# Recurrent attention and expert layer on one core: the last four expert tiles leave the pass over token order

## The reference

```python
xn = _layernorm(x)
# s: delta-rule linear attention, 4 heads, dk 128, dv 64
#    S = S + k_t (beta_t (v_t - k_t^T S))^T ;  o_t = q_t^T S
#    o = rmsnorm(o) * norm_w * silu(xn @ Wg) ;  s = o @ Wo
# f: mixture of 8 experts, each token goes to the one with the largest logit
#    h = square(relu(xn @ fc[e])) ;  f = h @ proj[e].T       (1024 hidden columns)
x = x + s * silu(f)
```

## Time and profile before

| | |
|---|---|
| median of three runs | 805.28 us (805.24 to 806.25) |
| profiled execution | 805.54 us, span 803.8 us |
| TensorE busy | 764.4 us (95%), granted clock 0.977 in the mean |
| DVE busy | 531.9 us (66%) |
| GpSimd busy | 393.3 us (49%) |
| ACT busy | 345.8 us (43%) |
| DMA | 116.25 MB, mean 145 GB/s |

### The profile page before, as it was taken

How to read it: one execution, slowest core, us unless ns; L and a number is a source line. 1 busy time by engine, 2 the same in 40 slices (tenths; PEclk the granted TensorE clock), 3 DMA queues, 4 the chain that set the end, 5 groups by cost and what they waited for, 6 DMA issues and landing times.

```text
span 803.8 us, 22106 instructions
## 1 busy us (share of the span) xinstructions
PE 764.4 (95%) x8970; PEld 649.3 (81%) x8970; DVE 531.9 (66%) x1159; ACT 345.8 (43%) x754; POOL 393.3 (49%) x407
## 2 busy tenths in 40 slices
PE   6969999999999999999999999999999999999953
PEld 5957888888888888888888888888787878788842
DVE  6786565655756556575565777676777676777577
ACT  4823434444443445344444444444443435354420
POOL 3725472535526354363544646364636474655411
PEclk9999999999999999999999999999999999999955
DMA  9608634425343253333623423232333333230087
GB/s 301 212 1 340 236 113 194 150 112 177 135 163 128 113 222 132 121 126 120 234 115 118 148 91 126 112 125 108 126 112 126 113 118 120 95 144 8 21 284 247
DMA packets 37748, 116.25 MB, mean 145 GB/s; under 512 B 3664, under 2 KB 24400, under 8 KB 27664
## 3 DMA queue, kind: packets, MB, share of 16 engines
q1 hardware_dynamic: 33904, 104.62, 35.3%
q0 software_dynamic: 3744, 10.23, 3.9%
HBM read 101.33 MB, written 13.50 MB: 143 GB/s over the span
## 4 chain that ended last, share of the span: by engine, by line
PE 88%; DVE 5%; POOL 3%; issue 2%; DMA 1%; another core or an unknown queue 1%; ACT 1%; DVEq 0%; POOLq 0%; SPq 0%
PE bank L466 18%; PE bank L477 16%; PE bank L542 7%; PE bank L510 7%; PE bank L495 6%; PE bank L442 4%; PE bank L440 4%; PE bank L441 4%; PE bank L681 4%; PE bank L577 3%; PE bank L587 3%; PE bank L597 2%; POOL ImM L2055 2%; PE bank L397 2%; PE bank L522 2%
## 5 line engine op out<-in xcount | busy, mean ns | idle before, releaser
L477 PE MATMUL bank<-wts,hT 128*128 128x256 f32 x624 | 172.2, 393 | 0.0
L466 PE MATMUL bank<-xsT,wts 128*128 128x128 f32 x1248 | 167.1, 281 | 0.1
L466 PEld LDWEIGHTS bank<-xsT,wts 128*128 128x128 f32 x1248 | 150.8, 192 | 10.9 <-issue 10.7
L1507 DVE TENSOR_TENSOR Pm<-bank,lvl_mask 128x256 f16<-128x256 f32 x192 | 72.5, 419 | 70.1 <-PE bank L577 69.2
L2036 POOL TENSOR_TENSOR XTl<-f_t,XTh 128x512 f16<-128x512 f32 x32 | 41.1, 1292 | 153.9 <-DVE XTh L1450 153.8
L1043 ACT CAST Z<-bank 128x256 f16<-128x256 f32 x192 | 63.2, 376 | 121.3 <-PE bank L597 121.3
L1518 DVE TENSOR_TENSOR M<-bank,M 128x256 f16<-128x256 f32 x192 | 73.3, 418 | 58.2 <-PE bank L587 57.5
L477 PEld LDWEIGHTS bank<-wts,hT 128*128 128x128 f32 x624 | 104.9, 191 | 7.0
L987 ACT ACTIVATE hT<-bank 128x512 f32<-128x512 f32 x78 | 46.7, 598 | 47.9 <-PE bank L466 47.6
L510 PE MATMUL bank<-xT,wq_sb 128*128 128x128 f32 x512 | 63.0, 276 | 0.0
L542 PE MATMUL bank<-wvg_sb,xT 128*128 128x512 f32 x128 | 62.9, 614 | 0.0
(11 more groups left out here) (213 smaller groups left out, 1930.5 us busy)
## 6 DMA issues: line engine op xcount, KB each, us to landing
wts<-in_fc SPq DMA_DIRECT2D x39, 1024.0 KB
wts<-in_pj SPq DMA_DIRECT2D x39, 1024.0 KB
wts<-in_x SPq DMA_DIRECT2D x10, 512.0 KB, 9.3
wts<-y_d SPq DMA_DIRECT2D x4, 1024.0 KB, 9.3
out_x<-wts SPq DMA_DIRECT2D x16, 256.0 KB, 2.2
xn_d<-wts SPq DMA_DIRECT2D x3, 1024.0 KB, 4.4
x_first<-in_x SPq DMA_DIRECT2D x4, 512.0 KB, 17.3
wts<-in_x SPq DMA_DIRECT2D x4, 256.0 KB, 3.5
```

Of the source, the lines that this page charges most:

```text
L466: ins = pe.matmul(psum[bank[n]][:, (c % 4) * P:(c % 4 + 1) * P], fcw[r][:, k, c * P:(c + 1) * P], xsT[:, k, :], start=(k == 0), stop=(k == ...
L477: ins = pe.matmul(psum[bank[0]][:, 0:D], hT[:, c, :], pjw[r][:, c, :], start=(c == 0), stop=(c == HC - 1))
L1507: dve.tensor_tensor(h4(Pm, b).rearrange("p h (n c) -> p h n c", c=s), half4(b).rearrange("p h (n c) -> p h n c", c=s), mask, ALU.mult).the ...
```

## The change

FIRST_TILES and STEPS cover 35 tiles instead of 37, so chunks 6 and 7 get two tiles each instead of three; tail() gets four tiles (64 units instead of 32), spread over the levels and the recurrence of chunk 15, 8 units behind O(15).

The four last tiles (LATE, 35 to 38) do not go through y_d in general. Their y stays in SBUF (in the room of wk). For them the rows of x (x_rows) and of s (s_rows, from a new DRAM copy s_d that SP writes chunk by chunk, keep_s) are gathered by GpSimd into the rooms of wq and wvg, DVE computes x + s * y (finish), and send_out scatters the rows to the output. Rows of the last chunk are an exception, since s of chunk 15 comes last: those rows of y are scattered into y_d (send_last), and chunk 15 is done in the pass. Rows that a scatter is to leave out have a number beyond the bound (late_rows computes both lists at the end of ramp()).

The pass itself goes chunk by chunk through four slots of `last` (x and y of 256 KB each) and covers all 16 chunks: y_d is filled with zeros at the start, so that tokens of late tiles get x alone from it, and the scatter overwrites them later. SP's loads, writes and keep_s stand in one list; a load waits until the slot's chunk before is written. The pass runs beside the levels of chunk 15, from chunk 0 on, before the experts have ended. Token rows in DRAM are numbered by sequence first (so xn_d is written in two DMAs for a part).

```diff
-        FIRST_TILES, STEPS = 2, [3] * 7 + [2] * 7
+        FIRST_TILES, STEPS = 2, [3] * 5 + [2] * 9
+        LATE = range(NT - 4, NT)
+        s_d = scratch("s_d", [NQ * P, D])
+        SKIP = 2 * NQ * P
+        SLOTS = 4
+        last = sb("last", [P, SLOTS, 2, B * D])
+        y_late, x_late, s_late = (w[:].rearrange("p k (z d) -> p (k z) d", d=D) for w in (wk_sb, wq_sb, wvg_sb))
@@ SP
+                    for b in range(B):
+                        sp.dma_start(xn_v[b, :, c0:c1], xa[:, b, c0:c1]).then_inc(rows_out, 16)
+                sp.dma_start(y_d[0:NQ * P].rearrange("(q p) d -> p q d", p=P),
+                             zeros.unsqueeze(1).to_broadcast([P, NQ, D])).then_inc(rows_out, 16)
+                sp.dma_start(s_v[NCH - 1], zeros.unsqueeze(1).to_broadcast([P, B, D])).then_inc(rows_out, 16)
...
+                def keep_s(c):
+                    At(sp, c).on(s_ok)
+                    sp.dma_start(s_v[c], s_all[:, 2 * c:2 * c + 2, :]).then_inc(rows_out, 16)
+                def load_x_of(c):
+                    if c >= SLOTS:
+                        sp.wait_ge(slot[c % SLOTS], written(c - SLOTS))
+                    sp.dma_start(x_of(c), xc_v[c]).then_inc(slot[c % SLOTS], 16)
+                def load_y(c):
+                    if c == 0:
+                        for r in range(RING):
+                            sp.wait_ge(y_out[r], 16 * len(range(r, LATE[0], RING)))
+                    if c == NCH - 1:
+                        sp.wait_ge(last_out, 16 * len(LATE))
+                    sp.dma_start(chunk_of(c), y_v[c]).then_inc(slot[c % SLOTS], 16)
+                def write(c):
+                    sp.wait_ge(out_ok, c + 1)
+                    sp.dma_start(o_v[c], chunk_of(c)).then_inc(slot[c % SLOTS], 16)
+                (order: load 0, next_weights(35), load 1 2 3, write 0 1, load 4, write 2, load 5 6,
+                 write 3 4, load 7, write 5, load 8 9, write 6, load 10, keep_s 13 14, write 7, load 11,
+                 write 8 9, load 12 13, write 10, load 14, write 11 12 13 14, load 15, write 15)
@@ TensorE tail: units behind each call
+  KS(14) 7, U(14) 6, M0(15) 2, Dm(0) 2, T(0) 2, L(1) 1, dS(14) Dm(1) 2, T(1) 2, L(2) 2, ogT_(14) Dm(2) 4,
+  T(2) 1, L(3) wo(14) Dm(3) 4, T(3) 2, L(4) 3, Dm(4) 2, T(4) KS(15) L(5) 2, Dm(5) 2, T(5) 2, F 2, Zc 2,
+  U(15) 4, O(15) 8, ogT_(15) wo(15)
@@ DVE
+                def late_rows():
+                    dve.wait_ge(rows_ok, 2)
+                    late = to_row[:, LATE[0]:NT]
+                    per_batch = NCH * P - P
+                    r(dve.tensor_scalar(in_last[:], late, per_batch, None, ALU.bitwise_and))
+                    r(dve.tensor_scalar(in_last[:], in_last[:], float(per_batch), float(SKIP), ALU.is_equal, ALU.mult))
+                    r(dve.tensor_tensor(out_row[:], late, in_last[:], ALU.add))
+                    dve.scalar_tensor_tensor(out=last_row[:], in0=late, scalar=float(SKIP), in1=in_last[:],
+                                             op0=ALU.add, op1=ALU.subtract).then_inc(rows_ok, 1)
+                def finish(j):
+                    n = LATE.index(j)
+                    At(dve, j).on(yg_ok)
+                    dve.wait_ge(late_in, 32 * len(LATE))
+                    r(dve.tensor_tensor(s_late[:, n], s_late[:, n], y_late[:, n], ALU.mult))
+                    dve.tensor_tensor(s_late[:, n], s_late[:, n], x_late[:, n], ALU.add).then_inc(late_ok, 1)
@@ DVE tail: weigh(c) and add_x(c) one or two between the halves of each level, from weigh(0) behind oss_(14)
+   ... Pm_(15, 3, 0) weigh(4) Pm_(15, 3, 1) add_x(4) dM(15, 3, 0) weigh(5) dM(15, 3, 1) add_x(5) S_l(14) weigh(6)
+   ... dM(15, 5, 1) add_x(8) R32(15) weigh(9) R_h Fr_ Fr_ add_x(9) R_l weigh(10) add_x(10) U_h U_l weigh(11)
+   add_x(11) weigh(12) oss_(15) add_x(12) og_(15) weigh(13) ... add_x(14) finish(35 to 38) weigh(15) add_x(15)
@@ ACT tail: ... dZf_(15) keep_y(37) y_sigmoid(37) relu(38) sq(38) osq(15) keep_y(38) y_sigmoid(38) ogTc(15) s_cp(15)
@@ GpSimd
+                def send_last(j):
+                    n = LATE.index(j)
+                    At(pool, j).on(yg_ok)
+                    pool.wait_ge(rows_ok, 3)
+                    pool.indirect_dma_start(
+                        out=y_d, out_offset=bass.IndirectOffsetOnAxis(ap=last_row[:, n:n + 1].bitcast(U32), axis=0),
+                        in_=y_late[:, n], in_offset=None, bounds_check=NQ * P - 1, oob_is_err=False).then_inc(last_out, 16)
+                def s_rows(j):
+                    At(pool, NCH - 1).on(*VGp)
+                    pool.wait_ge(rows_out, NORMAL_OUT + 16 * (NCH - 1))
+                    pool.indirect_dma_start(
...
+                def send_out(j):
+                    n = LATE.index(j)
+                    pool.wait_ge(late_ok, n + 1)
+                    for c in range(NCH - 1 - SLOTS, NCH - 1):
+                        pool.wait_ge(slot[c % SLOTS], written(c))
+                    pool.indirect_dma_start(
...
@@ GpSimd tail
+  x_rows(35) rows(37) x_rows(36) orn_(14) ogm(14) x_rows(37) x_rows(38) gate_y(35) rows(38) gate_y(36) ImM_ ImM_
+  send_last(35) s_rows(35) s_rows(36) send_last(36) s_rows(37) s_rows(38) gate_y(37) send_last(37) orn_(15)
+  ogm(15) gate_y(38) send_last(38) send_out(35 to 38)
```

More of the change, by code:

```diff
@@ new lines, in _ @@
+                load_x_of(0)
+                load_y(0)
+                next_weights(35)
+                load_x_of(1)
+                load_y(1)
+                load_x_of(2)
+                load_y(2)
+                load_x_of(3)
+                load_y(3)
+                write(0)
+                write(1)
+                load_x_of(4)
+                load_y(4)
+                write(2)
+                load_x_of(5)
+                load_y(5)
+                load_x_of(6)
+                load_y(6)
@@ new lines, in _ @@
+                write(3)
+                write(4)
+                load_x_of(7)
+                load_y(7)
+                write(5)
+                load_x_of(8)
+                load_y(8)
+                load_x_of(9)
+                load_y(9)
+                write(6)
+                load_x_of(10)
+                load_y(10)
+                keep_s(NCH - 3)
+                keep_s(NCH - 2)
+                write(7)
+                load_x_of(11)
+                load_y(11)
+                write(8)
@@ new lines, in _ @@
+                write(9)
+                load_x_of(12)
+                load_y(12)
+                load_x_of(13)
+                load_y(13)
+                write(10)
+                load_x_of(14)
+                load_y(14)
+                write(11)
+                write(12)
+                write(13)
+                write(14)
+                load_x_of(15)
+                load_y(15)
+                write(15)
+                for c in range(NCH - SLOTS, NCH):
+                    sp.wait_ge(slot[c % SLOTS], written(c))
@@ L1850, in tail @@
                     dM(15, 2, 1)
+                    weigh(3)
                     S_h(14)
-                    dM(15, 2, 0)
-                    S_l(14)
-                    R32(15)
-                    Pm_(15, 3, 0)
-                    Pm_(15, 3, 1)
-                    R_h(15)
-                    dM(15, 3, 0)
-                    dM(15, 3, 1)
-                    R_l(15)
+                    add_x(3)
+                    Pm_(15, 3, 0)
+                    weigh(4)
+                    Pm_(15, 3, 1)
@@ L2164, in tail @@
                 def tail():
-                    gate_y(37)
+                    x_rows(35)
+                    rows(37)
+                    x_rows(36)
                     orn_(14)
                     ogm(14)
-                    send_y(37)
-                    gate_y(38)
-                    send_y(38)
+                    x_rows(37)
+                    x_rows(38)
+                    gate_y(35)
+                    rows(38)
+                    gate_y(36)
                     ImM_(15, 0)
                     ImM_(15, 1)
+                    send_last(35)
+                    s_rows(35)
+                    s_rows(36)
+                    send_last(36)
+                    s_rows(37)
+                    s_rows(38)
+                    gate_y(37)
+                    send_last(37)
                     orn_(15)
                     ogm(15)
+                    gate_y(38)
+                    send_last(38)
+                    send_out(35)
+                    send_out(36)
+                    send_out(37)
+                    send_out(38)
                 ramp()
```

325 lines of the change are left out of this document (182 added, 143 removed).

## The result

The changed kernel takes 819.36 us (median of 4 runs, 818.78 to 819.85) against 805.5 us for the kernel before on the same chip: a ratio of 1.0167 (95% interval 1.0155 to 1.0179), 1.7% slower. The forecast was 789.7 us, and a range of 785 to 799. The profiled execution has a span of 817.1 us, 13.3 us more than before.

The account below looks back on a forecast made before the run. TensorE's work bounds the body; the serial chain of chunk 15 and the pass bound the last 40 us. Walked end 785.2, +2 queue, +1 contention: span 788.2; +1.74 - 0.26 gives 789.7 us, range 785 to 799.

Parts of the forecast that it names:

- The body: Expert steps before the tail: two steps go from three tiles to two, gaining 13.2 us, R32(14) at 727.4.
- load_y(0) waits for y_out of tiles 32 to 34, at about 731: Start of the pass on SP: the first y load waits for send_y(34), landing 2.6 us after issue; weigh(0) due at 739.
- TensorE's own work in the tail: Matmul work from R32(14) to O(15): 40.2 us at full clock, so O(15) would end at 767.6 without waits.
- the walk: Step-by-step reckoning of chunk 15's levels across engines, then the end: O(15) at 769.6, osq to 771.0, span end 785.2.
- The pass through four slots ... I take +2: Slot loads and writes in the tail: round 7.2 us empty; 11.3 MB need 30 to 32 us against 29, so +2.
- Rival B: Pass: a slot's round grows to 15.8 us, 3.95 a chunk, time 805.3 us; over 806.9 us given 0.05.
- No cost, and 18 us of room: SP's load of the last tile's weights behind load_y(0): 2.1 MB take 6 us, wanted at 761, nothing lost.
- The 2.0 us of waits (0.5 and 1.5) in the walk of chunk 15: TensorE's waits in the tail: 0.5 us before L(15, 3), 1.5 around F, putting O(15)'s end at 769.6.
- The signs: Marks for chunk 15: R32(15) at 757 to 761, TensorE over 90% busy, clock 1.0 until about 770.
- So the end stretch, 16.3 us before, stays 15.6: After O(15): send_last(38), load_y(15), last weigh and add_x end at 785.2; GpSimd's send_outs, beside that branch, at 783.9.
- Contention: VectorE slowed by GpSimd's 8 tensor operations in the tail: ends 0 and +4, taken as +1 us.
- Rival C: Tail: 14 indirect DMAs slow VectorE's weigh and add_x as GpSimd tensor operations do, +6, giving 795 us; chance 0.07.

Follow-up runs that it names:

- e8: Kernel before with only the four tiles moved to the tail, all rows through y_d and the old undivided pass behind them: 810.4 us, ratio 1.0060.
- e1: Changed kernel, but weigh and add_x write results into the room of s, so no load waits for a write's landing: 809.5 us, ratio 1.0039.
- e2: Changed kernel, but SP issues the loads of slots 1 to 3 ahead of the last tile's weights: 818.4 us, ratio 1.0153.
- e5: Changed kernel with both the edits of e1 and e2: 810.0 us, ratio 1.0061.
- e12: Changed kernel, slots as they were, with e9's order on VectorE, GpSimd and SP: 821.8 us, ratio 1.0209.
- e3: Changed kernel without the loads of chunks 4 to 15, all writes after the last add_x: 825.2 us (one run), its end not comparable.
- e9: e1 with most weighs moved behind chunk 15's levels, finish last, and some SP and GpSimd work reordered: 811.5 us, ratio 1.0064.
- e6: e5 without the four scatters of the late tiles' rows to the output: 803.3 us, ratio 0.9972.
- e7: Kernel before with a one-column copy on GpSimd behind the last add_x: 809.4 us, ratio 1.0048.
- e10: e9 without the four scatters of the late tiles' rows, nor the wait for them: 801.0 us, ratio 0.9938.
- e4: Kernel before with one unused GpSimd gather of 128 rows behind the last add_x: 811.6 us, ratio 1.0069.
- e11: e9 with finish ahead of weigh(15), load(15) ahead of write(12), weigh(8) ahead of oss(15): 811.0 us, ratio 1.0071.

## Why the prediction was wrong

**The body: right.** Forecast 13.2 us, measured 12.5 us at R32(14). The missing 0.7 is in the ramp or the first steps: R32(1) is at 148.39 us, 147.67 before. The ramp was taken as 0, with ends -1 and +1.

**"load_y(0) waits for y_out of tiles 32 to 34, at about 731": 8 us too early.** The kernel before has two scatters behind such a step, and the second, here less the 13.2 us of the body, is issued at 732.2:

```profile
745.39 0.98 POOL L2013 DMA_INDIRECT y_d<-y_sb,to_row  x1 [0.30 <-issue]
```

With the forecast's 2.6 us to its landing that is 734.8. In the change it was issued at 732.84 and landed 6.1 us later, at 738.9, behind the 2 MB of weights of tile 37 that SP had issued at 727.37 (share 1.00 from 730 to 734 us). What this late start cost at the end no run takes apart.

**TensorE's own work in the tail: right.** e8 has R32(15) at 759.48 and oss(15) at 769.37, where the walk had 757 to 761 and 771.0.

**"The pass through four slots ... I take +2": this is the step that failed.** The round was worked out once as 7.2 us empty, and then only the bytes were priced: 11.3 MB against what the queue can move. In the run the queue was not the bound over the tail (share 0.71, 217 GB/s); it was full only while the last weights passed (share 1.00 from 730 to 734 us and 0.98 from 744 to 756 us). What counted was the round as a latency: two landings (3.3 and 4.0 us in the median, 5 to 6 us in the worst ones of the chain from 780 us on), the turn on VectorE between them, and the turn in SP's one queue, where a load_x that waits for the landing of write(c) keeps every later write and load from being issued. That made 17 us of 7.2. Rival B, given 0.05, is this mechanism, with a round of 15.8 us as its mark and "landings of 6 to 7 us" as its condition. In the median the landings stayed below that, and the waits in the two program orders did the rest. In B's own terms the run went: load_y(0) at 738.95 and not 731, then 60.8 us to weigh(14) at 799.76, 4.05 a chunk (B has the time of the kernel before at 3.95), then 17.3 us to the end and not 13.5. My reason against B, that four slots hold only 2 MB, was about bytes again. Shown by e1 (the write's landing taken out of the round: -10 us), by e2 and e5 (a wait taken out comes back one round later) and by e12 (chunk 15 earlier by 18 us, the end of the pass by 0.8).

**"No cost, and 18 us of room" for next_weights(35), the weights of tile 38: wrong on the other side.** The room was computed for who uses the weights, not for who stands behind them. Their two MB went ahead of loads 1 to 3 in the queue, and weigh(1) waited 5.61 us at 750.05. e2 and e5 show that taking this wait away alone gains no more than 1 us of the end, because the wait came back in the slots.

**The 2.0 us of waits (0.5 and 1.5) in the walk of chunk 15: wrong while weighs stand in it.** The change has osq(15) at 788.64. In e3, with no load after load 3, it is still at 783.92, of which up to 7.3 us are the one wait at the start. VectorE "is as full as TensorE", the text said, and the walk should have charged for it: e9, with the weighs behind the levels, gets R32(15) 3.8 us behind e8. By e12 it cost 0.8 us of the pass here. The signs went with it: TensorE was not over 90% busy at clock 1.0 until 770 us. It stood 4.38 us, until 751.49, for VectorE's update of S behind weigh(1), and from 752 to 756 us its granted clock was 0.61, a mixture of its 1.2 and 2.4 GHz levels.

**"So the end stretch, 16.3 us before, stays 15.6": wrong, by GpSimd.** The four send_outs were forecast to be done at 783.9, "just beside" the other branch, and the end of the program to lie 2.6 us behind whatever came last. That holds for a write issued by SP (2.65 us in e6), not for work of GpSimd (6.7 us in e7 behind a copy of 0.19 us). The kernel before hid it, since its GpSimd stopped 10 us ahead of the end. In the change the last scatter is issued 8.7 us ahead of the end. Scatters and end together cost 6.7 us (e5 to e6), or 10.5 us where they stood later (e9 to e10).

**Contention: forecast +1, about right.** In the changed kernel weigh and add_x keep 0.69 us beside indirect DMAs. Three of them take longer, 1.6 us in all: 1.04 and 1.53 us beside ImM and 1.09 us beside gate_y. A pair of rows for each (timelines of GpSimd and VectorE), first the indirect DMA, then gate_y:

```profile
800.21 1.18 POOL L2219 DMA_INDIRECT y_d<-wk_sb,last_row  x1 [0.81 <-POOL wk_sb L2152]
```
```profile
800.49 0.69 DVE L1724 TENSOR_TENSOR last<-last 128x512 f32<-128x512 f32 x1
```
```profile
769.17 1.18 POOL L2152 TENSOR_TENSOR wk_sb<-wk_sb,y_sg 128x256 f32<-128x256 f32 x1 [10.19 <-ACT y_sg L1118]
```
```profile
769.80 1.09 DVE L1724 TENSOR_TENSOR last<-last 128x512 f32<-128x512 f32 x1
```

Rival C plays no part. The Trainium skill (GPSIMD Engine Reference, section Specifications) gives contention for VectorE's instructions with two SBUF inputs: the trace agrees for these two tensor operations of GpSimd, but weigh and add_x kept 0.69 us beside its indirect DMAs.

**The sum, mended.** 819.4 less 10 for the write's landing in the round (e1) less 6.7 for scatters and GpSimd's end (e5 to e6) is 802.7, and e6 has 803.3. Another 2.3 us come off with the order of e10. What is left between its 801.0 and the forecast of 789.7 was not taken apart by a run of its own. The start of the pass, 8 us late, is in it, and so is the queue, which moved 292 GB/s at a share of 0.94 from 740 to 790 us where the forecast took 350 to 375: once the slots turn faster, the bytes are a rival again, and no run here excludes them. For the last steps of e10 its trace shows this: ogm(15) ends at 781.3, not 774.6, in part because GpSimd stood 4.75 us for the landing of the kept s chunk in front of the orn, and load_y(15) landed at 794.0, not 780.8, with send_last(38) and that load taking 5 to 6 us each with other transfers under way and not 2.6. All of this is argued, not tested.

So no version of the change that I ran, with all its work in it, beats the kernel before; the best is e1, at 1.0039. The gain of the body is real: it is spent on slot rounds and on an end behind GpSimd.

## What to carry to other kernels

A ring of few buffers has to be priced as a latency: landing, turn on the engine, turn in the queue, landing, divided by the number of buffers (here 17 us over four slots, against 7.2 us reckoned from empty transfers). Bytes over bandwidth is only the lower bound, and in an in-order queue one wait for a landing delays all later issues. A chunk's result should leave from a room that is not the one its next load waits for. And before work of GpSimd is moved to the end of a program, its own end has to be counted; a stall that disappears in one round and returns in the next is the sign that the round, not the stall, is the bound. In this kernel that was so; when the round had been shortened (e1), the queue itself was nearly full.

## What the hardware showed that I had not expected

- The program's end lies 6.7 us behind the end of GpSimd's last operation, even one of 0.19 us (e7), 6.8 us behind that of a gather (e4: 803.1 to 809.9) and 7.6 to 7.7 us behind that of the last scatter (the change, e1, e5, e9, e11 and e12), but 2.65 us behind the last write issued by SP (e6). In both e4 and e7 SP waits 4.5 to 4.6 us at the last line.
- A 256 KB write that lands in 2.2 us in the old pass has a median of 4.0 us in the new one, at a lower mean rate of the queue (217 GB/s over the tail; 350 to 375 in the old pass). 256 KB loads took 2.9 to 3.3 us in the change and 5.7 to 7.4 in e1 (medians), where more of them were under way at once; yet the writes of e1 landed in 2.1 us. Why loads and writes differ so was not tested.
